# Turning an expert's sums one step later, and a third turn of the tokens of 64 rows instead of 128

## The reference

```
x   = layernorm(x)                                  # 4 blocks of 512 tokens, 128 features
att = softmax(-dist_sq(x @ U)) @ x                  # per block
ffn = silu(x @ sg) * (x @ su) @ sd                  # shared expert, 1024 wide, all tokens
    + routed                                        # 8 experts, 512 wide, top 2 of 8
# routed: an expert takes at most CAP = 320 tokens,
#   eout = (silu(xg @ rg) * (xg @ ru)) @ rd, weighted, added back to its tokens
out = x + att + ffn
```

## Time and profile before

| | |
|---|---|
| median of 3 runs | 159.84 us (159.69 to 160.55) |
| the profiled execution: time, span | 160.08 us, 158.6 us |
| PE / PEld busy | 152.1 us (96%) / 135.2 us (85%) |
| DVE / ACT / POOL busy | 118.4 (75%) / 104.6 (66%) / 80.9 us (51%) |
| granted TensorE clock | at its upper level (2.4 GHz) in all 40 slices |
| DMA | 20.72 MB, mean 131 GB/s |

### The profile page before, as it was taken

How to read it: one execution, slowest core, us unless ns; L and a number is a source line. 1 busy time by engine, 2 the same in 40 slices (tenths; PEclk the granted TensorE clock), 3 DMA queues, 4 the chain that set the end, 5 groups by cost and what they waited for, 6 DMA issues and landing times.

```text
span 158.6 us, 3106 instructions
## 1 busy us (share of the span) xinstructions
PE 152.1 (96%) x964; PEld 135.2 (85%) x964; DVE 118.4 (75%) x295; ACT 104.6 (66%) x218; POOL 80.9 (51%) x96
## 2 busy tenths in 40 slices
PE   6989998979999999999999999999999999999992
PEld 6957764978999988888888999999999999878992
DVE  4799959797933789999897777687687686645862
ACT  3359999959876488767866559899686566343200
POOL 7651300357777777877400002698988867354000
PEclk9999999999999999999999999999999999999999
DMA  4999999991111115456069300224142110019486
GB/s 121 267 287 116 172 287 310 342 306 60 55 51 50 50 43 162 109 156 187 12 162 253 130 0 2 102 71 129 35 114 62 50 46 33 29 27 261 110 265 197
DMA packets 26350, 20.72 MB, mean 131 GB/s; under 512 B 2301, under 2 KB 22296, under 8 KB 26336
## 3 DMA queue, kind: packets, MB, share of 16 engines
q1 hardware_dynamic: 24544, 17.89, 43.3%
q0 software_dynamic: 1792, 2.65, 5.3%
HBM read 12.36 MB, written 7.92 MB: 128 GB/s over the span
## 4 chain that ended last, share of the span: by engine, by line
PE 85%; DVE 7%; DMA 3%; SPq 1%; issue 1%; ACT 1%; DVEq 0%; ACTq 0%
PE bank L1147 15%; PE bank L1149 15%; PE bank L1148 15%; PE bank L1228 9%; PE bank L1295 7%; PE bank L1345 5%; PE bank L1347 5%; PE bank L1346 5%; DMA acc<-in_L_attn_x_dram 3%; PE bank L1213 3%; PE bank L1361 2%; PE bank L1372 2%; DVE stats L831 1%; DVE xnT_lo L868 1%; PE bank L1196 1%
## 5 line engine op out<-in xcount | busy, mean ns | idle before, releaser
L648 ACT ACTIVATE silu<-bank 128x512 f32<-128x512 f32 (+1 forms) x64 | 33.2, 521 | 29.6 <-PE bank L1149 29.2
L542 POOL DMA_INDIRECT slots_dram<-row,slot_i x32 | 34.8, 1087 | 12.8 <-issue 9.4
L975 DVE TENSOR_TENSOR bank<-bank,silu 128x320 f32<-128x320 f32 (+1 forms) x48 | 27.2, 566 | 15.7 <-ACT silu L648 12.5
L561 POOL DMA_INDIRECT routed_dram<-eo,xg x24 | 23.0, 957 | 11.6 <-DVE eo L1015 6.3
L981 DVE TENSOR_TENSOR hid_lo<-bank,hid_hi 128x320 fp32r<-128x320 f32 (+1 forms) x48 | 26.3, 548 | 0.0
L1147 PE MATMUL bank<-xnT_hi,sw_hi 128*128 128x512 f32 x62 | 25.4, 410 | 0.4 <-DVE hid_s L975 0.4
L1149 PE MATMUL bank<-xnT_hi,sw_lo 128*128 128x512 f32 x62 | 24.5, 396 | 0.0
L1148 PE MATMUL bank<-xnT_lo,sw_hi 128*128 128x512 f32 x62 | 24.5, 395 | 0.0
L656 ACT CAST hid_hi<-bank 128x320 fp32r<-128x320 f32 (+1 forms) x48 | 22.9, 477 | 0.0
L549 POOL TENSOR_TENSOR ew_lo<-sw_raw,ew_hi 128x1024 fp32r<-128x1024 f32 x3 | 7.2, 2409 | 20.7 <-ACT ew_hi L672 20.7
L1295 PEld LDWEIGHTS bank<-sd,hid_s 128*128 128x128 f32 x128 | 14.9, 192 | 1.0 <-issue 0.9
(11 more groups left out here) (185 smaller groups left out, 312.5 us busy)
## 6 DMA issues: line engine op xcount, KB each, us to landing
sw_raw<-in_L_ffn_rg_dram SPq DMA_DIRECT2D x8, 256.0 KB, 3.1
sw_raw<-in_L_ffn_ru_dram SPq DMA_DIRECT2D x8, 256.0 KB, 3.9
rd_raw<-in_L_ffn_rd_dram SPq DMA_DIRECT2D x8, 256.0 KB, 3.8
routed_dram<-fill SPq DMA_DIRECT2D x1, 2048.0 KB, 12.3
routed<-routed_dram SPq DMA_DIRECT2D x8, 256.0 KB, 4.1
slots_dram<-fill SPq DMA_DIRECT2D x1, 1300.0 KB, 13.6
xg<-slots_dram SPq DMA_DIRECT2D x8, 130.0 KB, 2.4
row<-row SPq DMA_DIRECT2D x1, 1024.0 KB, 8.7
```

The lines of the kernel that those rows point to most:

```text
L542: G.indirect_dma_start(slots_dram, bass.IndirectOffsetOnAxis(slot_i[:, k, t:t + 1], 0), row[:, t, 0:RW], None, bounds_check=E * CAP - 1, o ...
L561: G.indirect_dma_start(routed_dram, bass.IndirectOffsetOnAxis(xg[0:n, e % XB, r, 1:2].bitcast(I32), 0), eo[0:n, e % 2, r, :], None, bounds ...
L648: C.activation(silu[:, q % 2, 0:n], gate_bank(q)[:, 0:n], ACT.Silu).then_inc(silu_ready, 1)
L975: V.tensor_tensor(hid, up[:, 0:n], silu[:, q % 2, 0:n], ALU.mult).then_inc(hid_ready, 1)
```

## The change

Two edits. The turn of a finished job's sums, on TensorE and the work of VectorE that follows it (`block_sum` or `expert_out`), moves one step later in the list; ScalarE's copy stays where it is, and so does expert 7, which is turned in `CLOSE`. And the third transpose of `turn_slots` takes `TAIL` = 64 rows of `xg` and 64 columns of `ident`, so that it writes 64 columns. The bank's columns 320 to 383, which it no longer writes, are read by nobody.

```
+    def turned_after(step):
+
+        return job_after(step - 1)
...
-                elif job_after(q) is not None:
-                    of, n = JOBS[job_after(q)]
+                elif turned_after(q) is not None:
+                    of, n = JOBS[turned_after(q)]
                     if of == "block":
                         block_sum(n)
                     else:
...
                 for r in range(3):
-                    last = nc.tensor.transpose(turn_b[0][:, P * r:P * r + P], xg[:, e % XB, r, 2:RW], ident[:, :])
+                    n = P if r < 2 else TAIL
+                    last = nc.tensor.transpose(turn_b[0][:, P * r:P * r + n], xg[0:n, e % XB, r, 2:RW],
+                                               ident[0:n, 0:n])
                 last.then_inc(xg_turned, 1)
...
-                elif job_after(q) is not None:
-                    turn_out(job_after(q))
+                elif turned_after(q) is not None:
+                    turn_out(turned_after(q))
```

## The result

The changed kernel takes 164.0 us (163.91 to 164.12), the kernel before 160.05 us in the same series. The ratio is 1.0245 (1.0214 to 1.0276): 3.9 us slower. The forecast was slower, at 163.0 us, in a range of 161.0 to 164.2. The profiled execution took 164.05 us, with a span of 162.6 us where the kernel before has 158.6.

A forecast was written before the change was run, and what follows sets the result against it. TensorE was taken to bound the experts' steps, busy for all 48 us. 160.08 + 2.0 (narrow turns) + 1.3 (end) + 0 (middle) = 163.4 us; with that execution 0.24 above the median, 163.0 was put, range 161.0 to 164.2.

The forecast's parts named there:

- A turn costs 0.11 per transpose, and nothing at its borders: TensorE in the experts' steps: removing six borders between transposes and products gives 0; at 0.08 each, -0.5 us.
- the second rival: Removed borders give 0.08 us each and narrow turns 0.055 each: faster, 158.9 us; chance 0.04.
- The narrow turn: Third turn of the tokens on TensorE: the 64-row shape loses 0.25 us at each of eight turns, +2.0 us (1.4 to 2.8).
- The first rival: No gap at 64 rows; the end still moves and ScalarE's delay costs 0 to 0.7: 161.5 us; chance 0.12.
- The end: Return of the routed rows: expert 6's later scatters delay expert 7's and the loads, +1.3 us (0.8 to 2.3).
- The middle: GpSimd's and SyncE's queues for experts 0 to 5: the step of delay, 1.6 us, is covered on ScalarE and costs 0.
- The third rival: The gap is there, but TensorE's own lateness hides the cost of the end: 161.8 us; chance 0.10.

The follow-up runs named there:

- move_only: The changed kernel with the third turn of the tokens back at 128 rows and columns, so only the move is left; 162.09 us, ratio 1.0102.
- size96: The kernel before with a third turn of the tokens of 96 rows and 96 columns, nothing moved; 160.02 us, ratio 0.9994.
- only6: The kernel before with expert 6's sums alone turned one step later, tokens' turn at 128 rows; ratio 1.0108 (0.9991 to 1.0225), in the disturbed first series only.
- move_not6: As move_only, but expert 6 is turned where it was before; 160.79 us, ratio 1.0029.
- plain128: The kernel before with the tokens' third turn as an ordinary matmul with the identity, 128 rows and 64 moving columns; 161.90 us, ratio 1.0105.
- plain64: As plain128, but with 64 rows of both operands; 164.15 us, ratio 1.0263.
- small_twice: The kernel before with a 64-row third turn of the tokens issued twice in a row, nothing moved; 163.49 us, ratio 1.0223.
- narrow_only: The kernel before with the third turn of the tokens narrowed to 64 rows and columns, nothing moved; 162.94 us, ratio 1.0152.
- full_shapes: The kernel before with two of its own small shapes made full (rw_raw's transpose and the ranking's one-row matmul); 159.81 us, ratio 0.9964.

## Why the prediction was right

- **A turn costs 0.11 per transpose, and nothing at its borders.** Shown. The move removes six borders and nothing came back: in `move_only` the turns of tokens stand 5.93 and 5.92 us apart where nothing waits, as before, and the second rival had 0.08 for each border. Over all turns the distance grew by 0.3 us.
- **The narrow turn loses 0.25 us (0.17 to 0.35) at each of eight turns, 2.0 us in all.** The mechanism is shown: the gap ahead of the load, no gap at 96 rows or with 128 rows and 64 columns, one gap for two small turns. The size is 0.29 a turn, 2.3 us on TensorE. The nearest row of before has 8 rows; the group there was 0.04 cheaper. The choice of half over a quarter of the array fell on the right side, but little stood behind it. The load of 104 columns in the earlier trace rows has 128 rows (`128*104`) and says nothing of a small number of rows; what loses nothing with fewer than 128 rows is seen first in `size96`. The first rival is out.
- **The end, 1.3 us (0.8 to 2.3).** The mechanism is shown by `only6`'s trace and by `move_not6`. Its parts were dated well. Less the 2.2 us of TensorE, expert 6's scatter comes at 139.2 (139.26 foretold), the `k=0` loads at 143.9 (143.9), and the `k=1` loads at 150.2, near the upper end of 149.6 to 150.5, as the scatters of expert 7 did again land only behind the `k=0` loads (152.4 against 152.2). For DVE the sum is right almost to the number: 1.9 less its spare 0.57 is 1.3, and its last sum ends 1.2 us later. The term that was missing is the stores, which do not follow the additions one for one: they add 0.6, so that the trace has 1.8 us. (The upper bound of 2.3 leaves out the spare 0.57 that the lower one takes off; by that sum it is 1.7, and the trace lies above it.) The times put less on it. The move costs 1.6 us, and without expert 6 it costs 0.5, which leaves 1.2 (0.6 to 1.7).
- **The middle, 0.** Right for the changed kernel: its growth of 2.0 us over seven turns is all shape, and ScalarE's wait for the down weights stayed in its cover: it is 0.58 us at 119.84, where about 1 was foretold. The cover is TensorE's own lateness, as said, and without it the price is small: 0.3 us in `move_only`'s trace, 0.5 us in `move_not6`'s time, within the 0 to 0.7 of the first rival. The tokens of expert 7 are part of it: PEld waits 0.3 us for them in `move_not6`.
- **The third rival** is out as well. The lateness of TensorE moved the scatters along, and the end was not hidden.

Together 2.3 + 1.8 = 4.1 us, less 0.1 by which the changed kernel's trace was ahead at the first turn of tokens (82.7 against 82.8), are the 4.0 us between the spans. The forecast of 163.0 was 1.0 us low, by 0.3 at the turns and 0.5 at the end, and by 0.2 because the kernel before took 160.05 us beside it and 159.84 in the runs it started from.

One thing in the end is not settled. In `plain128`, `plain64`, `small_twice` and the second run of `narrow_only` the stretch behind TensorE's end is 0.4 to 0.8 us longer than in the kernel before, though nothing there was changed. In the first run of `narrow_only`, and in `size96`, `move_not6` and `full_shapes`, it isn't. It comes in two forms. In the second run of `narrow_only` and in `plain64` the `k=1` loads come late (DVE waits 2.46 us in the former), DVE's 0.57 us of spare time is used up, and the last sums stand together as in the changed kernel. In `plain128` and `small_twice` DVE still idles ahead of its last sum (0.70 and 0.85 us), and only the last stores take longer. So a part of what the changed kernel shows at its end can come without the move. A time of these kernels is good to some tenths of a us only, and for the cost of the end it is not settled whether the 1.2 us of the times or the 1.8 us of the trace is nearer.

## What to carry to other kernels

Where TensorE is the bound, a smaller matmul is not a cheaper one. Before an operand is cut to 64 rows or fewer (1, 8 and 64 rows cost time here, 96 did not), look in the trace for another small shape and measure from the full matmul before it to the second one behind; padding the operand with zeros to 96 or 128 rows may be the faster form, and what it saves has to be looked for at the end of the kernel too. And when a result is moved a step later because nobody is waiting for it there, follow it through each queue to the last reader: of nine moved turns eight cost 0.5 us together and one 1.2 us, the one whose transfers meet the last expert's.

## What was not expected of the hardware

The second of two small transposes costs less than a full one. In `small_twice` it adds 0.06 us, where full transposes stand 0.11 apart; so within a run of 64-row transposes the small size does pay, and only the way in and out, 0.29 us against a full one, makes it a loss. It does not hold for the ordinary matmuls of `plain64`. There two of 64 rows stand in one group, and it takes 0.92 us, 0.15 more than the 0.77 with one small transpose; a second small matmul of that kind is no cheaper than a full one.
